# Three ring slots, two more resident tiles, a plain first product and a third filter applied to whole chunks in a graph kernel

## What is computed

```python
h = relu(adj @ (x @ W1) + b1)
h = relu(adj @ (h @ W2) + b2)
x = layernorm(x + h)
f1 = adj @ x @ V1
f2 = adj @ adj @ x @ V2
f3 = adj @ adj @ adj @ x @ V3
out = layernorm(x + (f1 + f2 + f3) / 3)
```

## Time and profile before

| | us |
|---|---|
| median of three runs | 253.12 (252.58 to 253.63) |
| the profiled execution, its own time | 252.85 |
| its span | 251.1 |
| TensorE busy | 244.2 |
| VectorE busy | 202.7 |
| ScalarE busy | 191.9 |
| granted clock of TensorE, mean | 0.994 |

### The profile page before, as it was taken

The page is one execution under the profiler, slowest core; times in us unless marked ns, Lnnn a source line. Parts: engine busy times, 40 slices in busy tenths (PEclk is TensorE's granted clock), DMA queues, the critical chain, the costliest instruction groups (busy, mean ns, idle before and its releaser), DMA issues.

```text
span 251.1 us, 3737 instructions
## 1 busy us (share of the span) xinstructions
PE 244.2 (97%) x1132; PEld 202.9 (81%) x1132; DVE 202.7 (81%) x396; ACT 191.9 (76%) x335; POOL 16.3 (6%) x23
## 2 busy tenths in 40 slices
PE   8999999999999999999999999999999999999991
PEld 8788888888888888886888888888888888888881
DVE  0999889896789889897888869776876767798865
ACT  2998899886868887878778787767777777678950
POOL 1000000000003031120000000000000000012232
PEclk9999999999999999999999999999999999999997
DMA  6999999920000000000043112100000000301102
GB/s 238 386 387 385 387 386 387 397 115 0 0 3 1 1 0 3 0 0 1 0 123 50 52 31 69 17 0 1 1 3 0 0 0 3 84 1 42 43 3 84
DMA packets 22532, 23.12 MB, mean 92 GB/s; under 512 B 11888, under 2 KB 12784, under 8 KB 22384
## 3 DMA queue, kind: packets, MB, share of 16 engines
q1 hardware_dynamic: 22224, 22.55, 26.4%
q10 hardware_dynamic: 288, 0.33, 0.4%
HBM read 20.51 MB, written 2.36 MB: 91 GB/s over the span
## 4 chain that ended last, share of the span: by engine, by line
PE 92%; DVE 3%; ACT 2%; issue 1%; POOLq 0%; POOL 0%; DVEq 0%; ACTq 0%
PE filters L445 19%; PE filters L438 19%; PE filters L439 19%; PE pair L445 9%; PE pair L438 9%; PE pair L439 9%; PE weighted L413 3%; ACT ring_high L581 1%; PE filters L454 1%; DVE ring_low L706 1%; PE turned L415 1%; PE pair L384 1%; DVE operand_low L662 1%; POOLq L143 0%; POOL rstd L371 0%
## 5 line engine op out<-in xcount | busy, mean ns | idle before, releaser
L706 DVE TENSOR_TENSOR ring_low<-adj,ring_high 128x512 fp32r<-128x512 f32 x240 | 159.7, 687 | 30.9 <-ACT ring_high L581 28.1
L581 ACT ACTIVATE ring_high<-adj 128x512 fp32r<-128x512 f32 x240 | 148.1, 629 | 31.6 <-PE filters L439 14.8
L438 PE MATMUL filters<-ring_high,operand_low 128*128 128x512 f32 x156 | 61.8, 396 | 0.0
L445 PE MATMUL filters<-ring_low,operand_high 128*128 128x512 f32 x156 | 61.0, 391 | 0.2 <-DVE ring_low L706 0.2
L439 PE MATMUL filters<-ring_high,operand_high 128*128 128x512 f32 x156 | 60.8, 390 | 0.0
L445 PEld LDWEIGHTS filters<-ring_low,operand_high 128*128 128x128 f32 x156 | 29.3, 188 | 7.0 <-DVE ring_low L706 0.9
L439 PEld LDWEIGHTS filters<-ring_high,operand_high 128*128 128x128 f32 x156 | 29.3, 188 | 5.7
L438 PEld LDWEIGHTS filters<-ring_high,operand_low 128*128 128x128 f32 x156 | 29.3, 188 | 5.6
L445 PE MATMUL pair<-ring_low,operand_high 128*128 128x512 f32 x84 | 32.9, 392 | 0.2 <-DVE ring_low L706 0.2
L438 PE MATMUL pair<-ring_high,operand_low 128*128 128x512 f32 x84 | 33.1, 393 | 0.0
L439 PE MATMUL pair<-ring_high,operand_high 128*128 128x512 f32 x84 | 32.7, 390 | 0.0
(11 more groups left out here) (84 smaller groups left out, 207.4 us busy)
## 6 DMA issues: line engine op xcount, KB each, us to landing
adj<-a_t SPq DMA_DIRECT2D x48, 256.0 KB, 9.7
resident_raw<-a_t SPq DMA_DIRECT2D x16, 256.0 KB, 9.7
scratch<-turned_blocks SPq DMA_DIRECT2D x5, 256.0 KB, 2.0
turned_rows<-scratch SPq DMA_DIRECT2D x20, 64.0 KB, 2.5
nodes<-x_rows SPq DMA_DIRECT2D x1, 1024.0 KB, 11.6
lead<-lead_in SPq DMA_DIRECT2D x3, 256.0 KB, 3.4
out_rows<-nodes SPq DMA_DIRECT2D x3, 256.0 KB, 2.4
lead<-lead_in ACTq DMA_DIRECT2D x1, 192.0 KB, 3.0
```

The lines of the kernel that those rows point to most:

```text
L438: nc.tensor.matmul(bank, y_low, a_high, start=first, stop=False)
L445: used = nc.tensor.matmul(bank, y_high, a_low, start=False, stop=last)
L581: nc.scalar.activation(ring_high[:, n % RING, :], source, ACT.Copy).then_inc(high_ready, 1)
L706: nc.vector.tensor_tensor(ring_low[:, n % RING, :], source, ring_high[:, n % RING, :].bitcast(F32), ALU.subtract).then_inc(low_ready, 1)
```

## The change

- The ring has three slots. Tiles (1,5) and (2,5) are resident as well: 46 tiles are streamed, 18 resident.
- The first step, (0,0,0), is one plain fp32 product of the unsplit tile with an unsplit block of `x @ W1`, which ScalarE copies to `first_row`. It is no item of the ring and doesn't wait for the split of x. X_SPLIT puts groups 2 and 3 before steps 5 and 9, not 1 and 3.
- V3 becomes a third lift. At the wide step of hop 3, chunks 0 to 2, `third_filter` makes six products: three as before, and three for V3 into the bank `weighted`. ScalarE evacuates that bank one step later, and the result goes by blocks as in hop 2. (3,3) keeps its post.
- The evacuation of a chunk in hops 2 and 3 is no longer pulled forward to its wide item. LATE makes the operand's low one item sooner, and OVERHANG is 13.
- Everything listed with RING moves with it from four to three items.

The diff, cut to its core:

```diff
-GROUPS = 4
-STREAMED = TILES // GROUPS - 1
-BLOCKS = GROUPS * STREAMED
-RING = 4
+EVERY = 4
+ALSO = ((1, 5), (2, 5))
+RING = 3
...
+THIRD = 2
+THIRD_WIDE = range(3)
...
-X_SPLIT = (0, 0, 1, 3)
+X_SPLIT = (0, 0, 5, 9)
+PLAIN = (0, 0, 0)
...
-BY_BLOCKS = {(2, 0): 17, (2, 1): 18, (2, 2): 16, (2, 3): 17, (4, 0): 14}
-POSTS_AFTER = {(3, 1): 6, (4, 1): 9, **BY_BLOCKS}
+BY_BLOCKS = {(2, 0): 17, (2, 1): 18, (2, 2): 16, (2, 3): 17, (3, 0): 20, (3, 1): 20, (3, 2): 19, (4, 0): 14}
+POSTS_AFTER = {(4, 1): 9, **BY_BLOCKS}
...
+def streamed(c, k):
+    return k == WIDE or (k % EVERY != EVERY - 1 and (c, k) not in ALSO)
...
+def in_ring(step):
+    return streamed(*step[1:]) and step != PLAIN
...
-LATE = {"stats": (1, 4), "moments": (2, 5), "shift": (4, 7), "apply": (5, 6, 8, 9), "high": 10, "low": 12}
+LATE = {"stats": (1, 4), "moments": (2, 5), "shift": (4, 7), "apply": (5, 6, 8, 9), "high": 10, "low": 11}
...
-def evacuation_item(hop, c):
-
-    item = BEFORE[end_of(hop, c)] + RING
-    return min(item, BEFORE[STEPS.index((hop, c, WIDE))]) if hop in LIFTS else item
+def evacuation_step(hop, c):
+
+    if hop == 3 and c in THIRD_WIDE:
+        return STEPS.index((hop, c, WIDE)) + 1
+    return end_of(hop, c)
...
 def evacuations(n):
     return [(hop, c) for hop in range(HOPS) for c in range(CHUNKS)
-            if (hop, c) != (HOPS - 1, CHUNKS - 1) and evacuation_item(hop, c) == n]
+            if (hop, c) != (HOPS - 1, CHUNKS - 1) and BEFORE[evacuation_step(hop, c)] + RING == n]
...
+            for c in THIRD_WIDE:
+                store_blocks(3, c)
+                load_rows(3, c)
...
-                elif hop in (0, 3) and c > 0:
+                elif hop == 0 and c > 0:
                     pe.wait_ge(operand_low_ready, operands(hop, c - 1))
...
                 nc.tensor.matmul(bank, y_low, a_high, start=first, stop=False)
                 used = nc.tensor.matmul(bank, y_high, a_high, start=False, stop=False)
+                if hop == 3 and k == WIDE and c in THIRD_WIDE:
+                    third_filter(bank, c, n)
+                    return
...
+            def third_filter(bank, c, n):
+
+                z_high, z_low = ring_high[:, n % RING, :], ring_low[:, n % RING, :]
+                product = weighted[:].rearrange("p t d -> p (t d)")
+                if c:
+                    pe.wait_ge(chunk_evacuated, 3 * CHUNKS + c)
+                nc.tensor.matmul(product, lift_low[:, THIRD, :], z_high, start=True, stop=False)
+                nc.tensor.matmul(product, lift_high[:, THIRD, :], z_high, start=False, stop=False
+                                 ).then_inc(high_used, 1)
+                pe.wait_ge(low_ready, n + 1)
+                nc.tensor.matmul(bank, lift_high[:, LIFTS[3], :], z_low, start=False, stop=False)
+
+                nc.tensor.matmul(product, lift_high[:, THIRD, :], z_low, start=False, stop=True).then_inc(low_used, 1)
+
+            def plain_product():
+                hop, c, k = PLAIN
+                pe.wait_ge(first_row_ready, 1)
+                pe.wait_ge(arrival(c, k), 16)
+                nc.tensor.matmul(sums_of(hop, c), first_row[:], block(c, k), start=True, stop=False)
...
-                act.wait_ge(chunk_summed, hop * CHUNKS + c + 1)
+                source = sums_of(hop, c)
+                if hop == 3 and c in THIRD_WIDE:
+                    act.wait_ge(low_used, item_of(hop, c) + 1)
+                    source = weighted[:].rearrange("p t d -> p (t d)")
+                else:
+                    act.wait_ge(chunk_summed, hop * CHUNKS + c + 1)
...
+                if g == 0:
+                    nc.scalar.activation(first_row[:], product_of(g)[:, 0, :], ACT.Copy).then_inc(first_row_ready, 1)
```

More of the change, by code:

```diff
@@ L46 @@
 STRIPS = P // BLOCK
-BY_BLOCKS = {(2, 0): 17, (2, 1): 18, (2, 2): 16, (2, 3): 17, (4, 0): 14}
-POSTS_AFTER = {(3, 1): 6, (4, 1): 9, **BY_BLOCKS}
-def streamed(k):
-    return k % (STREAMED + 1) != STREAMED
+BY_BLOCKS = {(2, 0): 17, (2, 1): 18, (2, 2): 16, (2, 3): 17, (3, 0): 20, (3, 1): 20, (3, 2): 19, (4, 0): 14}
+POSTS_AFTER = {(4, 1): 9, **BY_BLOCKS}
+def streamed(c, k):
+    return k == WIDE or (k % EVERY != EVERY - 1 and (c, k) not in ALSO)
+PLACES = [(c, k) for c in range(CHUNKS) for k in range(TILES)]
+STREAMED = [place for place in PLACES if streamed(*place)]
+RESIDENT = [place for place in PLACES if not streamed(*place)]
+def in_ring(step):
+    return streamed(*step[1:]) and step != PLAIN
 ALL = range(TILES)
@@ L192, in graph_layers @@
         weighted = psum("weighted", [P, TPC, D])
-        adj_in = [[sem(f"adj_in{c}_{n}") for n in range(BLOCKS)] for c in range(CHUNKS)]
-        resident_in = [[sem(f"resident_in{c}_{j}") for j in range(GROUPS)] for c in range(CHUNKS)]
+        adj_in = {(c, k): sem(f"adj_in{c}_{k}") for c, k in PLACES}
         lead_first = sem("lead_first")
@@ L231, in graph_layers @@
         out_stored = sem("out_stored")
-        block = ctx.enter_context(nc.Block())
+        engines = ctx.enter_context(nc.Block())
         half_tiles = TPC // HALVES
@@ L273, in arrival, with block, resident @@
         def arrival(c, k):
[L274 to L277, removed]
+            return adj_in[c, k]
+        def block(c, k):
+            return adj[:, STREAMED.index((c, k)), :]
+        def resident(parts, c, k):
+            return parts[:, RESIDENT.index((c, k)), :]
         def residents(c, k):
             order = tile_order(0)
-            return sum(not streamed(tile) for _, _, tile in order[:order.index((0, c, k)) + 1])
+            return sum(not streamed(chunk, tile) for _, chunk, tile in order[:order.index((0, c, k)) + 1])
         def product_of(g):
@@ L287, in product_of @@
             return (turned if g == 2 else weighted)[:]
-        @block.sync
+        @engines.sync
         def _(sp):
             def load(c, k):
[L292 to L296, removed]
+                place = block(c, k) if streamed(c, k) else resident(resident_raw, c, k)
+                sp.dma_start(place, a_t[c, :, k, :]).then_inc(arrival(c, k), 16)
             for g, (first, last) in enumerate(X_GROUPS):
@@ L347, in _ @@
             sp.wait_ge(out_stored, 16 * (CHUNKS - 1 + HALVES))
-        @block.gpsimd
+        @engines.gpsimd
         def _(pool):
@@ L372, in _ @@
                                         ).then_inc(rstd_ready, 1)
-        @block.tensor
+        @engines.tensor
         def _(pe):
@@ L434, in tile_products @@
                 else:
[L435 removed]
+                    a_high, a_low = resident(resident_high, c, k), resident(resident_low, c, k)
                     if hop == 0:
@@ L468, in _ @@
                             post(h, chunk)
+                if (hop, c, k) == PLAIN:
+                    plain_product()
+                    continue
                 if hop == 0 and c == 0:
                     for g, (first, _) in enumerate(X_GROUPS):
-                        if first == k:
+                        if max(first, 1) == k:
                             pe.wait_ge(operand_low_ready, g + 1)
@@ L494, in _ @@
             add_sums(3).then_inc(post_multiplied, 1)
-        @block.scalar
+        @engines.scalar
         def _(act):
             def evacuate(hop, c):
-                act.wait_ge(chunk_summed, hop * CHUNKS + c + 1)
+                source = sums_of(hop, c)
[4 more added lines that the diff above has]
+                    act.wait_ge(chunk_summed, hop * CHUNKS + c + 1)
                 before = (hop, c - 1) if c else (hop - 1, CHUNKS - 1)
@@ L568, in _ @@
                     nc.scalar.activation(lift_high[:], lift_raw[:], ACT.Copy).then_inc(lift_high_ready, 1)
-                if i < STREAMED:
+                if in_ring((hop, c, k)):
                     visits(n)
@@ L579, in _ @@
                             act.wait_ge(arrival(c, k), 16)
-                        source = adj[:, c, j * STREAMED + i, :]
+                        source = block(c, k)
                     nc.scalar.activation(ring_high[:, n % RING, :], source, ACT.Copy).then_inc(high_ready, 1)
                     n += 1
-                elif hop == 0:
+                elif hop == 0 and not streamed(c, k):
                     act.wait_ge(arrival(c, k), 16)
-                    nc.scalar.activation(resident_high[:, c, j, :], resident_raw[:, c, j, :], ACT.Copy
+                    nc.scalar.activation(resident(resident_high, c, k), resident(resident_raw, c, k), ACT.Copy
                                          ).then_inc(resident_high_ready, 1)
@@ L597, in _ @@
             act.dma_start(out_rows[:, last_tiles(1), :], nodes[:, last_tiles(1), :]).then_inc(out_stored, 16)
-        @block.vector
+        @engines.vector
         def _(dve):
@@ L654, in operand_tiles @@
                 source = {1: nodes[:, part, :], 2: turned[:]}.get(hop, weighted[:])
-                if hop == 2 and (hop, c) in BY_BLOCKS:
+                if (hop, c) in BY_BLOCKS:
                     source = turned_rows[:, (hop + 1) % 2, part, :]
@@ L704, in _ @@
```

(8 more changed lines are left out.)

43 lines of the change are left out of this document (22 added, 21 removed).

## The result

The changed kernel takes 254.74 us (median of five runs, 254.55 to 255.14) against 253.12 before; the ratio is 1.0067, 95% interval 1.0051 to 1.0083. It is slower by 1.6 us, a little more than what a measurement of this kernel can tell from no change.

A forecast was written before the change was run, and what follows sets the result against it. TensorE, busy 244.2 of 251.1 us, was taken as the bound. The terms -0.82 + 0.50 - 0.66 + 1.36 + 0.3 + 0.6 gave +1.28 on the profiled 252.85: 254.1 us, range 252.2 to 255.6.

The forecast's parts named there:

- case A: Whole kernel: the sum of the terms as it stands, 254.1 us, own range 253.3 to 254.9; chance 0.42.
- Head: Kernel start: the plain product takes 0.87 us and tile 1 starts earlier, -0.82 us.
- Hop 0: At (0,1,9) and (0,1,10): landings don't move, so part of the head's gain is given back, +0.50 us.
- Third filter: Hop 3, chunks 0 to 2: posts of 0.90 go, three wide products of 0.68 come, -0.22 each, -0.66 us.
- The bounce of (3,1): Hop 3: rows read back 0.7 us late against 1.1 spare in the ring; no cost, bounded at 0.7.
- Ends of (2,2) and (2,3): Hop 2, wide tiles: VectorE's low comes late, +0.69 and +0.67, together +1.36 us; no third such place.
- Norms of hop 1: Near 117 us: a loss of 0.78 goes, new losses of 1.1 come ahead of it, +0.3 us.
- Norms of hop 4: Last chunk: two misses, by 0.1 and 0.4, with restarts +0.6 us (bounds 0 and 1.2).
- B: Rival, (1,2,12) to (2,1,6): hop 1's exchanges don't fit in three slots, 2.6 for 1.1, 255.6 us; chance 0.18.
- C: Rival, faster: lows called late are made in gaps, since 16 operations went, 251.4 us; chance 0.15.
- D: Rival: hop 0 doesn't dip, the norms hide, only the two ends of hop 2 remain, 252.6 us; chance 0.20.
- E: Rival, head: the plain product waits or runs at the lower clock, tile 1 no earlier, 254.9 us; chance 0.05.

The follow-up runs named there:

- e4: Kernel before with three slots instead of four, and of the rest of the change only LATE's low and OVERHANG: 255.9 us, ratio 1.0109.
- e3: Changed kernel with the head of before (first tile split, x groups split before steps 0, 0, 1 and 3): 254.28 us, ratio 1.0040.
- f2: Kernel of f1 with the head of before (all tiles split, early x splits): 252.29 us, ratio 0.9967.
- e1: Changed kernel with the operand halves of (2,1) and (2,2) listed later, at 20 and 19 for 18 and 16: 253.44 us, ratio 1.0022.
- e2: Changed kernel with the rows of (3,1) taken up four items later (25 for 20): 253.15 us, ratio 1.0008.
- f1: Changed kernel with the moved due times of both e1 and e2: 251.9 us, ratio 0.9958.
- f3: Kernel of f1 with the third filter as before (posts in hop 3, no wide tile or bounce): 252.65 us, ratio 0.9981.
- f4: Kernel of f1 with four slots, 16 residents and the lows one step later in the list: 252.08 us, ratio 0.9959.

## Why the prediction was right, and where its sum was off

The forecast was 254.1 by case A, whose own range, up to 254.9, holds the measured 254.74. The bound of 0.5% lies at 1.27 us; the loss of 1.6 is a little beyond it, in the part of A that was counted as slower. The largest cause is the one named: three slots leave a tile less lead, and the ends of hop 2 open. The second largest was not foreseen, and the sum came near because two misses upwards (+1.3, +0.35) met two downwards (-0.86, -0.3). That the time came out only 0.6 above the forecast is in part luck.

- **Head**: right, -0.80 for -0.82. The plain 512-column product took 0.86, as twice the 256-column row had it.
- **Hop 0**: 0.35 too small, and the place holds for this execution only. The working took the 0.43 spare of one product and left its low where it was, ending at 28.15; it ended at 28.47. A landing had moved: (0,1,8) came at 24.73, not 23.25, so the operand's high had to be made behind it. The four traces in which (0,1,8) is the first tile to come late lose 0.5 to 0.9 from there to (0,1,12): the changed kernel, e4, and e3 and f2, whose TensorE has the head of before and isn't early. The five others lose 0.11 at most there. In e1, e2, f1 and f3 the head's gain goes earlier, 0.4 to 0.8 of it within chunk 0. In all five traces with this head and three slots (0,0,12) starts 3.30 to 3.36 after the landing of (0,0,10). So it is the landings that take the gain back, as the prediction had it, but where and how much varies from one execution to the next.
- **Third filter**: right for the post, -0.18 each for -0.22, and f3 gives 0.6 for all. That a post in three slots opens a wait of its own (0.31) wasn't seen.
- **The bounce of (3,1)**: the step that failed, "no cost, bounded at 0.7"; it cost 1.3. ScalarE came for the rows when forecast, 15.6 us behind the wide tile of (3,0) for 15.5. The rows were in at 17.6 for 16.2. SP issued the store at 182.13, 0.46 after the turn's end at 181.67, because the four reads of (3,0) held its queue until 182.09; then the store took 2.75 and the reads' issue 3.17, where one row of hop 2, 2.0 and 2.59, had been used for both. Against the ring's 1.1 spare 2.04 of wait leaves 0.94, and three restarts of 0.11 make 1.27. The prediction's bound was no bound: it moved the lateness with a single sample of a transfer whose time varies by 1.2, and let the spare absorb it first. The trace of before had the warning: from the store's issue to the last landing its five bounces took 6.5, 6.7, 7.1, 7.9 and 8.0 us (the last two are a pair, stored 2.7 apart), and the sum used the 6.7. With 8.0 the rows are in at 17.5. e2 shows the cause.
- **Ends of (2,2) and (2,3)**: right, +1.39 for +1.36, with the releaser, the places and the size. e1 takes away 1.1 to 1.4. "I find no third" held.
- **Norms of hop 1**: the gain of 0.78 was right, and f4 brings it back; the 1.1 of new losses ahead of it was wrong. The low of (1,3,13) and the exchange at (2,0,1) did not open waits; only some 0.3 was lost up to (2,1,3). I had costed the three slots as if VectorE had kept its load: e4 shows such losses, 1.0 by (2,1,7), with 16 residents. The two residents gave the lows their lead back.
- **Norms of hop 4**: +0.29 for +0.6; one miss of 0.14, not two.

**The rivals.** B, the exchanges of hop 1 in three slots, did not come in the changed kernel. It exists in small in e4. The Trainium skill (SBUF — State Buffer, "SBUF: two separate sides") would have GpSimd's power steps hold VectorE's lows there; the trace disagrees, the low's mean stays at 0.69 while the power step's is 0.96. The steps of 1.0 are those that start while one of VectorE's 128x512 operations is already running; two, at 80.70 and 92.26, start with VectorE idle and take 0.69, though a low begins 0.35 and 0.28 into them, and that low takes its 0.69 too. C failed as argued: at the ends VectorE is held by order, not by load. D and E failed too: hop 0 did dip, and the plain product started at 8.49, with a granted clock of 1.00 in that stage. The waits looked for in hop 3 under "wrong" did come.

## What to carry to other kernels

A due-time list that was tuned at one ring depth is part of the ring: take a slot away and the items just in front of an urgent one have to be placed again. Three moved due times turned this change from 1.6 us lost into 1.1 won. When a result makes a round trip through memory, put its use behind the worst landing seen, not the usual one; here four items later cost nothing. And price a saving at the head only up to the next place where the stream waits for its data, with several executions: here one execution differs from the next by more than what is left of the saving.

## What the runs showed of the hardware

One transfer is as late as its slowest lane. In the changed kernel 15 of the 16 completions of the store of (3,0) came from 178.16 to 178.32 and the last at 179.47, 1.15 later. The packet records have one 8 KB packet of the instruction queue at 177.30 there, 0.78 us long, between the store's own. The pattern is the same in e1, e2 and f1 (last lane 0.96 to 1.12 behind the others, packet of 0.66 to 0.80). In e3 and f2 the packet took 0.49 and 0.44 and all lanes came within 0.3. The store of (3,1) is another case: its 16 completions came between 184.42 and 184.86, counted from its issue all 0.5 to 0.7 later than in e3, and no such packet is near. What was near are the reads of (3,0), issued up to 182.09, right ahead of it, and landed at 184.16; in e3 0.7 lay between. In hop 0 a 16 KB packet at 22.56 us took 1.13, and from then on the last lane of each tile came 1.3 to 1.5 behind the rest; before, with the packet at 22.98, the first tile so held back was the next one. That these packets are what held the lane is read from the times alone: no run moved one. The start of the packet doesn't order the traces, either: at 22.98 and 23.05 (0,1,9) is the first late tile, at 23.06 and 23.28 it is (0,1,8). So what decides which tile is held, and with it the place of hop 0's loss, stays open.

The Trainium skill (DMA: Bandwidth & Descriptors, "Anatomy of one DMA — SWDGE (gpsimd) path") gives, for transfers issued by GpSimd, a fixed cost of about 2.0 us, most of it until the last byte is confirmed, and a time for the bytes beside it. These stores are issued by SP, 256 KB each: in e3 they took 2.12 and 2.02 in all, in the changed kernel 3.20 and 2.75. By the fit that this section of the Trainium skill gives for that other path, 256 KB would take 2.6 us, an estimate. So the usual store here stays below it, and the late ones above: the figure bounds nothing.
